# A two-layer block kernel on one core: attention's steps planned with new durations, and the ends of its batches ranked last

## The reference

```python
x = x + 0.5 * L0_ffn(ln(x))   # silu(w1 h) * (w2 h), then gelu(h1 .), gelu(h2 .), w3; width 512
x = x + L0_attn(ln(x))        # linear attention, 32 latent features
x = x + 0.5 * L0_ffn(ln(x))
x = x + 0.5 * L1_ffn(ln(x))   # 8 experts of rank 64, the two best of a batch's first token
x = x + L1_attn(ln(x))        # 16 heads of 8, rotary, causal softmax, output projection
x = x + 0.5 * L1_ffn(ln(x))
```

## Time and profile before

| | us |
|---|---|
| median of 3 runs | 768.81 |
| lowest, highest | 764.74, 771.1 |
| the profiled execution | 767.41 |
| its span, first to last instruction | 763.1 |
| mean granted TensorE clock | 0.971 of full speed |

### The profile page before, as it was taken

One profiled execution on the slowest core, in us unless ns is written; L12 is line 12 of the kernel. 1 busy time (PEld: TensorE's weight loads), 2 busy tenths in 40 slices (PEclk: granted clock), 3 DMA queues, 4 the chain that ended last, 5 costly groups with the idle time before them and its releaser, 6 DMA issues.

```text
span 763.1 us, 14946 instructions
## 1 busy us (share of the span) xinstructions
PE 684.7 (90%) x5660; PEld 500.7 (66%) x5660; DVE 525.3 (69%) x1306; ACT 502.8 (66%) x830; POOL 311.1 (41%) x433
## 2 busy tenths in 40 slices
PE   2889999999999999999999989798879798889886
PEld 1667777778777777777787766555446355555565
DVE  3745455777657655678677768988699785979543
ACT  2767687977788867979777953346645556557541
POOL 2201121133413130224263475646668474545543
PEclk9889999999999999999999999999989898999999
DMA  9100000000110000000011123215534344332111
GB/s 294 46 1 1 0 1 1 1 0 2 38 46 0 1 1 1 0 2 1 26 58 43 43 87 107 85 47 180 169 122 149 132 152 156 102 132 99 66 57 29
DMA packets 47088, 47.29 MB, mean 62 GB/s; under 512 B 3240, under 2 KB 41128, under 8 KB 46760
## 3 DMA queue, kind: packets, MB, share of 16 engines
q1 hardware_dynamic: 47016, 46.33, 18.4%
HBM read 23.51 MB, written 22.54 MB: 60 GB/s over the span
## 4 chain that ended last, share of the span: by engine, by line
PE 47%; DVE 23%; ACT 12%; issue 6%; DMA 6%; SPq 3%; POOL 2%; POOLq 1%; DVEq 0%; ACTq 0%
PE PSA L787 16%; PE PSA L791 15%; DVE MX L1094 8%; DMA LC<-do 4%; DVE LC L1115 3%; ACT PSA L1146 3%; DVE G L1017 2%; PE PSA L804 2%; SPq L1340 2%; PE PSA L959 2%; ACT G L1142 2%; DVE RA L1087 1%; PE PSA L900 1%; ACT ah L1153 1%; ACT L1142 1%
## 5 line engine op out<-in xcount | busy, mean ns | idle before, releaser
L1240 POOL TENSOR_TENSOR RS<-VE,MHALF 128x4 f32<-128x4 f32 x48 | 49.3, 1028 | 229.7 <-DVE VE L999 229.5
L787 PE MATMUL PSA<-ah,WH 128*128 128x512 f32 x320 | 131.3, 410 | 5.7 <-DVE al L1022 3.0
L1094 DVE TENSOR_REDUCE MX<-PSA 128x6 f32<-128x768 f32 x128 | 116.9, 943 | 13.8 <-PE PSA L922 13.7
L791 PE MATMUL PSA<-al,WH 128*128 128x512 f32 x320 | 125.4, 392 | 0.0
L1146 ACT ACTIVATE PSA<-PSA,SC 128x512 f32<-128x512 f32 x128 | 84.7, 661 | 57.4 <-PE PSA L791 56.7
L1222 ACT ACTIVATE PB<-PSA 128x768 f32<-128x768 f32 x128 | 99.2, 820 | 18.3 <-PE PSA L946 18.1
L787 PE MATMUL PSA<-bh,WH 128*128 128x512 f32 x256 | 105.7, 413 | 4.0 <-DVE bl L1022 2.5
L791 PE MATMUL PSA<-bl,WH 128*128 128x512 f32 x256 | 101.2, 395 | 0.0
L1288 POOL TENSOR_SCALAR_AFFINE_SELECT PB<-PB 128x512 f32<-128x512 f32 x128 | 79.7, 636 | 43.1 <-ACT PB L1222 41.7
L1022 DVE TENSOR_TENSOR al<-PSA,ah 128x512 fp32r<-128x512 f32 x64 | 44.2, 691 | 68.8 <-ACT ah L1153 68.8
L787 PEld LDWEIGHTS PSA<-ah,WH 128*128 128x128 f32 x320 | 60.2, 188 | 22.0 <-DVE al L1022 5.2
(11 more groups left out here) (122 smaller groups left out, 1411.1 us busy)
## 6 DMA issues: line engine op xcount, KB each, us to landing
do<-OT SPq DMA_DIRECT2D x15, 512.0 KB, 6.7
KS<-dk SPq DMA_DIRECT2D x32, 192.0 KB
QS<-dq SPq DMA_DIRECT2D x32, 192.0 KB
dk<-CB SPq DMA_DIRECT2D x16, 192.0 KB, 2.3
dq<-CB SPq DMA_DIRECT2D x16, 192.0 KB, 2.4
X<-in_x SPq DMA_DIRECT2D x8, 256.0 KB, 6.9
dk<-CB SPq DMA_DIRECT2D x16, 128.0 KB, 2.2
dq<-CB SPq DMA_DIRECT2D x16, 128.0 KB, 2.4
```

Source lines behind the costliest of these rows:

```text
L787: e.matmul(o, WH[:, col:col + 128], hi, start=first, stop=False)
L791: return e.matmul(o, WH[:, col:col + 128], low, start=False, stop=last)
L1094: e.tensor_reduce(MX[:, u % 2, :, :].rearrange("p t (l g) -> p l t g", l=2)[:, :, :, g], PSA[:, b:b + 2, 0:384].rearrange("p l (t k) -> p ...
L1240: e.tensor_tensor(RS[:, i, :], VE[:, i, :], MHALF[:, :], ALU.pow).then_inc(g_rs, 1)
```

## The change

Prices in `TAKES` are raised: the peaks (0.88 to 1.7 us of DVE), the transfer of `reloc` (3.6 to 5.0), of `max_out` (3.2 to 3.8), of `ot_out` (6.6 to 7.5) and of `vl_in` (3.7 to 4.7). Statistics get a second price of 1.9 us, `stat_late`, which `put` takes once one feed-forward stream has ended. QUEUED goes from 1.5 to 1.2, LEAD from 14 to 24. The end of a batch gets rank 6.6, behind the second pass (6) and behind the first pass at either of its ranks (5.5, 6.5). No instruction is added or removed but the fillers, whose number follows from the plan.

```diff
+    "stat": [("V", 1.39, 1.48)], "stat_late": [("V", 1.9, 2.0)], "power": [("G", 1.02, 1.03)], ...
-    "rest1": [...], "reloc": [("S", 2.95, 2.95), ("D", 3.6)],
+    "rest1": [...], "reloc": [("S", 2.95, 2.95), ("D", 5.0)],
-    "pass1": [("P", 0.35, 0.51), ("V", 0.868, 0.95)], "peak": [("V", 0.88, 1.0)],
-    "max_out": [("P", 0.22, 0.29), ("V", 0.2, 0.27), ("S", 1.18, 1.18), ("D", 3.2)],
+    "pass1": [("P", 0.35, 0.51), ("V", 0.868, 0.95)], "peak": [("V", 1.7, 1.8)],
+    "max_out": [("P", 0.22, 0.29), ("V", 0.2, 0.27), ("S", 1.18, 1.18), ("D", 3.8)],
-    "weigh": [("P", 0.79, 0.86), ("A", 0.27, 0.38)], "ot_out": [("S", 0.45, 0.45), ("D", 6.6)],
-    "vl_in": [("S", 1.12, 1.12), ("D", 3.7)], "recip": [("V", 1.66, 1.74)], ...
+    "weigh": [("P", 0.79, 0.86), ("A", 0.27, 0.38)], "ot_out": [("S", 0.45, 0.45), ("D", 7.5)],
+    "vl_in": [("S", 1.12, 1.12), ("D", 4.7)], "recip": [("V", 1.66, 1.74)], ...
-QUEUED = 1.5
-LEAD = 14
+QUEUED = 1.2
+LEAD = 24
@@ put
-        for i, (eng, us, *way) in enumerate(TAKES[name]):
+        late = name + "_late" if self.dead and name + "_late" in TAKES else name
+        for i, (eng, us, *way) in enumerate(TAKES[late]):
@@ probs
-        self.add(5, self.fin(u, self.last_weigh))
+        self.add(6.6, self.fin(u, self.last_weigh))
```

## The result

The changed kernel takes 742.9 us (median of 4 runs, 741.1 to 744.9), the kernel before 767.5 (764.7 to 771.1): a ratio of 0.9677, 95% interval 0.9627 to 0.9727. The direction was right, the size was not: 24.6 us instead of the 8.8 forecast against the median shown, and 742.9 is outside the range of 750 to 774.

The account below looks back on a forecast made before the run. DVE was taken to lead the 250 us first-pass stretch, with 36.3 us idle to win, and latency the end. From 767.4, terms of -6, -1.5, -1.5 and +1.5 gave 759.9, forecast 760 us, range 750 to 774.

Parts of the forecast that it names:

- (d): Peaks and late statistics on DVE: new prices overcount where old ones undercounted; 0 us, bounds 8 lost and 5 won.
- (a): First-pass stretch: reciprocals laid up to 1.9 us later cut DVE's LC waits by 7 us; with the rank, 6 counted.
- (c): Query loads: the higher reloc price shortens PE's 3.67 us wait before a first pass; 1.5 us won, bounds 0 and 7.
- (g): After 712 us on POOL: ends go behind selects, shortening ACT's 3.20 us wait for a weighing; 1.5 us won.
- (h): End of the run: longer first-pass lead leaves more exponentials, capped by buffers; 1.5 us lost, bounds 9.4 lost and 4 won.
- (e): Second pass laid 0.6 us later by max_out's price, covered by two batches of lead; 0 us, at most 10.
- (f): Passes laid only with DVE or ACT backlog under 1.2 us, starving neither; 0 us, bounds 2 each way.
- Other waits take the gain: Rival: DVE's saved time turns up in other waits, largest on first-pass matmuls; 766 us, same, chance 0.22.
- The lead lengthens the end: Rival: after the last first pass, 8 more exponentials cost 9.4 us; 775 us, slower, chance 0.15.
- Shuffled plans: Rival: plan's clocks drift so far by 700 us that prices only shuffle the order; 767 plus or minus 4, chance 0.13.
- The share of 0.08 left below the range: Chance of under 750 us for the whole kernel: all waits gone at once and a shorter end.
- the signs for the forecast: Expected in the trace: LC waits under 5 us, QS under 2, last first pass some 8 sooner, no picks before selects.

Follow-up runs that it names:

- the nudged control: Kernel before with peak 1.7 and stat_late 1.9, plus max_out's transfer at 3.3 instead of 3.2: 749.2 us (0.9785).
- rank and limits: Kernel before with QUEUED 1.2, LEAD 24 and rank 6.6 for ends of batches, all prices old: 762.6 us (0.9964).
- DVE's prices: Kernel before with only peak raised to 1.7 and stat_late to 1.9: 742.2 us (0.9707).
- the sum on PE: Kernel before with 20.8 us added to PE's price of the 64 weighings (0.79 to 1.115 us each): 754.5 us (0.9871).
- the nudged kernel before: Kernel before with only the ot_out price moved from 6.6 to 6.7: 770.7 us (1.0062).

## Why the prediction was wrong, step by step

**Step (d), the step that failed.** It took peak and stat_late at 0 us, "as engines run when they can whatever the plan thought", with bounds of 8 lost and 5 won. They alone won 22.7 us, 15.6 in the nudged control. The mistake was to price a mispricing by its own length (16 x 0.3; the bound even left the statistics out, 15 x 0.2). The plan fixes the order across engines, so an engine doesn't run when it can but when its list lets it, and the plan's DVE clock was short of the chip by 28 us, not by 5, since it also lacks the waits that it doesn't foresee. Prices above the measured mean stand in for these: with the means of the trace the drift is 14.2 us (753.0), with the change's values 0.7 and 3.1 (742.2 and 749.2). The rows for this reading were in the trace: 30.8 us of weight loads waiting behind DVE in three rows, while DVE itself was idle for 36. I had read DVE's waits and not PE's. The sign named for this step, more fillers while DVE idles, came only by half: from 462 to 712 us the matmuls of L930 (L931 after) rose from 382 to 473, and DVE idled less.

The Trainium skill (SBUF — State Buffer, "Who interferes with whom") says that a DVE instruction with two SBUF inputs contends with a GpSimd instruction that reads SBUF. The trace before agrees: of the 48 parts of peaks the 21 longer than 0.3 us all ran beside POOL instructions, and the 16 without one beside them took 0.192 us at most. The middle part reads only one tile, which that sentence doesn't cover, and spreads as well. For the time it changed nothing that these runs show. After the change the three parts still spread as in the earlier trace rows:

```profile
L1103 DVE TENSOR_TENSOR MX<-MX x16: 108/166/1151, 477.1 to 697.2; 128x16 f32<-128x16 f32 x16
L1105 DVE TENSOR_SCALAR HM<-MX x16: 180/181/637, 477.3 to 697.6; 128x32 bf16<-128x32 f32 x16
L1107 DVE SCALAR_TENSOR_TENSOR HM<-MX,HM x16: 191/372/1142, 477.5 to 697.8; 128x32 bf16<-128x32 f32 x16
```

Most peaks are far shorter than 1.7 us, and the price works all the same, as slack.

**Steps (a) and (c), the transfers.** Counted 6 with the rank, and 1.5. The transfers alone gave 7.1 us (4.6 inside the span), and the wait for LC fell to 4.5 us, as the text wanted (under 5). The size fits, but it lies within a draw, and the cause doesn't hold: the wait fell to 2.8 us by rank and limits, to 5.5 by DVE's prices and to 5.7 by the sum on PE, all with the old price of LC, and the rank-and-limits run shows that filling it buys little by itself. PE's matmuls waited 2.6 us for queries instead of 5.1, not under 2.

**Step (g), picks before selects.** Wrong as a mechanism. They are still there in the changed kernel, POOL and then ACT:

```profile
699.22 0.40 POOL L1272 TENSOR_TENSOR WB<-PT,GS 128x128 f32<-128x128 f32 x1 [0.94 <-issue]
...
701.71 2.40 POOL L1289 TENSOR_SCALAR_AFFINE_SELECT PB<-PB 128x512 f32<-128x512 f32 x4
...
704.28 0.38 ACT L1231 ACTIVATE OT<-PSA 128x256 f32<-128x256 f32 x1 [3.23 <-PE PSA L960]
```

ACT waits 3.23 us as it did before (3.20). The stretch after the last reduce got 5.1 us shorter nevertheless; it is 18 to 20 us in most runs with new DVE prices, with the new rank or without (18.9 with DVE's prices alone), so the rank isn't the cause by itself.

**Step (h), LEAD.** Taken at 1.5 lost; with the rank and new prices it is 0 (743.0 against 742.9). With the old prices and LEAD, QUEUED and rank new, 22 exponentials were left, and the stretch took 27.5 us, 3.9 more than before; which of the three does it wasn't tried. The rival's price existed in that run, but the gain elsewhere covered it. The 1.17 us for an exponential, from which step (h) and the rival took 9.4 us, stands in no row: 23.5 us for 16 are 1.47 each. **(e), (f)** weren't tried alone. Two pairs differ in QUEUED only: DVE's prices and rank, 746.9 with 1.5 and 752.6 with 1.2, and all prices and rank with LEAD 14, 743.9 and 743.0. Both are within a draw, so nothing speaks against (f)'s 0.

**Rivals.** "Other waits take the gain" happened to the rank-and-limits run, whose gain went into waits for queries, and in the run with the transfers alone, where it went into waits for first-pass matmuls, not to the change. "The lead lengthens the end" happened in part there. "Shuffled plans" is right as to the scatter, 4 to 7 us, and had named the drift of the plan's clock, but took it for a reason why better prices would do nothing; that is wrong as to the whole. The share of 0.08 left below the range was the case that came. Of the signs for the forecast, the last first pass ended 14 us sooner (696.8 against 711.0) instead of some 8, and 15 exponentials were left instead of 16 to 19.

## What to carry to other kernels

Where a planner orders in-order engines, compare its clock with the trace step by step before costing waits one by one: the engine whose steps fall ever further behind the plan is the one to look at first, and what is at stake is nearer to the whole drift than to the error of one price, here 28 us against 5. Rounding the price of the leading engine's work up, beyond its mean, took the drift away here, as the surplus stood in for waits; that it beats true prices, or slack elsewhere, is less sure. And test a plan's edit together with a meaningless nudge of it: here one was worth 4 to 7 us, as much as the four transfer prices.

## What was not expected of the hardware

The device time outside the span, first to last instruction, is a property of the order: 4.0 to 5.0 us in every run of the old order, under either text, and 1.7 to 2.2 in all but one of the others (3.1 to 3.3), the nudged kernel before among them. No row of the trace shows where it lies.
